# Two delta-rule attentions of a long kernel: the products with W give way to a product and a subtraction ahead of the inverse

## The chip, the cores and the metric

The kernel runs on one core of one Trainium2 chip. The metric is the device time of one execution in microseconds (us), taken as the median of several runs. TensorE (PE) multiplies matrices, VectorE (DVE) and ScalarE (ACT) do elementwise work, GpSimd (POOL) does small powers and indirect transfers, and SyncE (SP) issues transfers. Each engine works through its own instructions in order and waits on semaphores for the others.

## The reference, cut to what matters

The whole program is eight stages in sequence (attention and feed-forward of four layers). Two of them hold a delta rule in chunks: the first stage, `l0_attn`, and the fifth, `l2_attn`. There are 8 sequences of 512 rows, 4 heads, and chunks of 128 rows in the kernel (the mathematics doesn't depend on the chunk). For each head and chunk of `l0_attn`:

```
inv   = (I + strictly_lower(kb @ k.T))^-1        # kb = k * beta, v is already v * beta
u     = inv @ v
w     = inv @ kb
u_adj = u - w @ S                                # S: the state, key columns x value columns
out   = q @ S + lower(q @ k.T) @ u_adj
S     = S + k.T @ u_adj
```

`l2_attn` is the same with a decay in each row: what it takes from the state (by k and by q) is multiplied by `from_start`, the decay since the start of the chunk, and S shrinks by `whole` from one chunk to the next. Its value columns are 64 a head (256 in all); in `l0_attn` they are 32 a head (128 in all).

## The kernel before, in words

All products are in f32. A matmul of f32 shows in the trace as two MATMUL records ("x2"), so four heads are "x8".

**Lanes.** Each stage takes its 8 sequences as units in two lanes, A (units 0, 2, 4, 6) and B (1, 3, 5, 7), so there are four rounds of A and B. A unit is cut into phases, the places of `yield` in the code, and each engine's program is written in one order by `weave`: a phase of A, then a phase of B, and so on, with A one phase ahead. No engine can change this order.

**Chunks and pairs.** A unit has four chunks of 128 rows, worked on as two pairs. For a pair, `score_pe` forms kb·k and q·k for all heads of both chunks (L782), and `levels_pe` builds the inverses from small blocks, level by level (L800, L808, L816, L825, L833; the last two are `left6`, L840, and `right6`, L847). After `right6` DVE writes the last block of the inverse (L926, the step `whole`). The transposed inverse of each head is XT, the masked q·k is AT.

**After the inverse, per pair.**

- phase `wt`: `wt_pe` forms the transposed W of both chunks, 8 matmuls with 32 output rows each (L934), and ACT moves them to SBUF with a minus sign (L941, `wt_moved`).
- phase `u` of a chunk: `values_pe` accumulates -W·S (one matmul, L947) and inverse·v of four heads (L949) in bank 1; behind it, a matmul of q with S (L1107 in `l0_attn`, L2664 in `l2_attn`). ACT copies bank 1 to U (L955, `values`). In `l2_attn` DVE scales q·S (L2886).
- phase `out` of a chunk: k.T·U into bank 3 (L1110, L2667; `added`), AT·U of four heads (L1112, L2671; `out`). DVE keeps the head blocks of bank 3 and adds them to S (L1330 and L1332; L2890 and L2892; `state`), ACT (`l0_attn`, L1198) or DVE (`l2_attn`, L2895) takes the output (`got`).

S is zero in chunk 0. Written by lane, the order of the phases at the end of pair 0 is:

```
A.right6 B.left6 A.wt B.right6 A.u0 B.wt A.out0 B.u0 A.u1 B.out0 A.out1 B.u1 (A's next) B.out1
```

Pair 1 has the same order, with chunks 2 and 3. In `l0_attn` A's next phase is the score of pair 1 (L782) or, after chunk 3, a transpose (L422); in `l2_attn` it is `between`, whose decays DVE prepares (L2865) for a product of PE (L2650), or the squares of the output (ACT L2766, DVE L2899).

**Filters in `l0_attn`.** Through the levels of pair 0, PE also forms a long convolution (L1249) in bank 1 of both lanes, and DVE copies it out in eight copies (L1278, mark `filtered`). DVE has them in its order by phases: the last four behind A's `whole` and ahead of B's `whole`. PE waits for the last of them before the values of chunk 0.

**Decay in `l2_attn`.** Before the pairs, DVE multiplies the rows `kb` by `from_start` (L2860) and `krow` by `to_end` (L2861), once a unit.

Of the kernel before, what the change touches and what calls it, by code (L numbers as in the profile page):

```python
# [7 lines left out]
ALU = mybir.AluOpType  # L8
# [3 lines left out]
P = 128  # L12
# [676 lines left out]
HEADS, DK = 4, 32  # L689
# [51 lines left out]
def delta_phases(pair):  # L741

    names = [f"score{pair}"]
    for n in range(1, SMALL_LEVELS + 1):
        names += [f"left{pair}_{n}", f"right{pair}_{n}"]
    names += [f"turn{pair}", f"left{pair}_6", f"right{pair}_6", f"wt{pair}"]
    for chunk in (2 * pair, 2 * pair + 1):
        names += [f"u{chunk}", f"out{chunk}"]
    return names


class Delta:
# [5 lines left out]
    def __init__(self, c, arena, dv, scaled):  # L758
        self.c, self.dv, self.width = c, dv, HEADS * dv
        self.NT, self.AT, self.X, self.XT, self.T1 = (arena.take(2, HEADS, P) for _ in range(5))  # L760
        self.WT = arena.take(2, P)
# [12 lines left out]
        self.qS = arena.take(HEADS, dv) if scaled else None  # L774
# [155 lines left out]
    def wt_pe(self, pe, u, pair, kbe):  # L930
        for j in range(2):
            pe.wait_ge(*u.dve.at(f"whole{pair}"))
            for hh in range(HEADS):
                made = pe.matmul(u.banks[0][DK * hh:DK * hh + DK, cols_of(j)], chunk_heads(kbe, 2 * pair + j)[:, hh, :],  # L934
                                 self.XT[:, j, hh, :])
        made.then_inc(*u.pe.step(f"wt{pair}"))
        yield f"wt{pair}"

    def wt_act(self, act, u, pair):
        act.wait_ge(*u.pe.at(f"wt{pair}"))  # L940
        act.mul(flat(self.WT), u.banks[0][:, 0:2 * P], -1.0).then_inc(*u.act.step(f"wt_moved{pair}"))  # L941
        yield f"wt{pair}"

    def values_pe(self, pe, u, j, vb):

        bank, dv = u.banks[1], self.dv
        pe.matmul(bank[:, 0:self.width], self.WT[:, j, :], self.S, start=True, stop=False)  # L947
        for hh in range(HEADS):
            made = pe.matmul(bank[:, hh * dv:(hh + 1) * dv], self.XT[:, j, hh, :], vb[:, hh, :], start=False,  # L949
                             stop=hh == HEADS - 1)  # L950
        return made

    def values_act(self, act, u, chunk):
        act.wait_ge(*u.pe.at(f"u{chunk}"))
        act.copy(all_heads(self.U[chunk % 2]), u.banks[1][:, 0:self.width]).then_inc(*u.act.step(f"values{chunk}"))  # L955
# [59 lines left out]
class L0Attn:  # L1015
# [39 lines left out]
    def pe(self, pe, u):  # L1055
# [31 lines left out]
        for pair in range(CHUNKS // 2):  # L1087
# [8 lines left out]
            yield from d.wt_pe(pe, u, pair, m.kb)  # L1096
            for j in range(2):
                chunk = 2 * pair + j
                pe.wait_ge(*u.act.at(f"wt_moved{pair}"))
                if chunk > 0:  # L1100
                    pe.wait_ge(*u.dve.at(f"state{chunk - 1}"))
# [4 lines left out]
                d.values_pe(pe, u, j, chunk_heads(m.vb, chunk)).then_inc(*u.pe.step(f"u{chunk}"))  # L1106
# [41 lines left out]
    def act(self, act, u):  # L1148
# [36 lines left out]
        for pair in range(CHUNKS // 2):  # L1185
# [7 lines left out]
            yield from d.wt_act(act, u, pair)  # L1193
            for chunk in (2 * pair, 2 * pair + 1):
                d.values_act(act, u, chunk)
# [85 lines left out]
    def dve(self, dve, u):  # L1281
# [36 lines left out]
        for pair in range(CHUNKS // 2):  # L1318
# [7 lines left out]
            yield f"wt{pair}"  # L1326
            for chunk in (2 * pair, 2 * pair + 1):
                yield f"u{chunk}"
# [1251 lines left out]
class L2Attn:  # L2580
# [16 lines left out]
    def pe(self, pe, u):  # L2597
# [47 lines left out]
        for pair in range(CHUNKS // 2):  # L2645
# [9 lines left out]
            yield from d.wt_pe(pe, u, pair, m.kb)  # L2655
            for j in range(2):
                chunk = 2 * pair + j
                pe.wait_ge(*u.act.at(f"wt_moved{pair}"))
                if chunk > 0:
                    pe.wait_ge(*u.dve.at(f"state{chunk - 1}"))  # L2660
                else:
                    pe.wait_ge(*u.dve.at("cleared"))
                d.values_pe(pe, u, j, chunk_heads(m.vrow, chunk, L2_ATTN_DV)).then_inc(*u.pe.step(f"u{chunk}"))
# [30 lines left out]
    def act(self, act, u):  # L2694
# [54 lines left out]
        for pair in range(CHUNKS // 2):  # L2749
# [10 lines left out]
            yield from d.wt_act(act, u, pair)  # L2760
            for chunk in (2 * pair, 2 * pair + 1):
                d.values_act(act, u, chunk)
# [29 lines left out]
    def dve(self, dve, u):  # L2792
# [67 lines left out]
        dve.tensor_tensor(heads_of(m.kb), heads_of(m.kb), over(m.from_start, DK), ALU.mult).then_inc(*u.dve.step())  # L2860
        dve.tensor_tensor(heads_of(m.krow), heads_of(m.krow), over(m.to_end, DK), ALU.mult).then_inc(*u.dve.step("weighed"))  # L2861
        yield "keys"
        for pair in range(CHUNKS // 2):
# [18 lines left out]
            yield f"wt{pair}"  # L2882
            for chunk in (2 * pair, 2 * pair + 1):
                dve.wait_ge(*u.pe.at(f"carried{chunk}"))
# [973 lines left out]
```

## Time and profile before

| | |
|---|---|
| median of 3 runs | 6054.68 us (6027.5, 6054.68, 6063.11) |
| profiled execution | 6045.51 us, span 6044.2 us |
| mean granted TensorE clock | 0.736 of full speed |
| busy, share of the span | PE 70%, PE weight loads 54%, DVE 50%, ACT 32%, POOL 14% |
| chain that ended last, by engine | PE 50%, DVE 29%, ACT 12%, issue 4% |

The profiled execution took 1.3 us more than its span, and lies 9.2 us under the median. The page cuts the span into 40 equal slices of 151 us: `l0_attn` lies in slices 1 to 7 and `l2_attn` in slices 20 to 27.

### The profile page before, as it was taken

What the parts mean: (1) busy time and instruction counts of PE and PEld (TensorE: products, weight loads), DVE (VectorE), ACT (ScalarE), POOL (GpSimd) and SP (SyncE); (2) the same over time, 40 slices, a digit from 0 to 9 for tenths busy, and PEclk for the clock granted to TensorE, in tenths of its full rate; (3) what the DMA queues carried; (4) which work ended last, traced back from release to release, by engine and by line L of the source; (5) the groups of instructions that cost most, each with busy time, mean ns of one, the idle gap of its engine ahead of it and who ended that gap; (6) DMA issues with size and microseconds to landing.
All of it is one profiled execution on the core that took longest, in us unless ns stands there. A gap on an engine that the chain in (4) does not pass through costs nothing.

```text
span 6044.2 us, 94874 instructions
## 1 busy us (share of the span) xinstructions
PE 4245.8 (70%) x39740; PEld 3259.7 (54%) x39740; DVE 2998.6 (50%) x7965; ACT 1939.8 (32%) x4236; POOL 817.7 (14%) x600
## 2 busy tenths in 40 slices
PE   6686968468878887855475766757767677766298
PEld 5574847345555565544364655634444445445277
DVE  4445363335555555565446455455565555555333
ACT  2233132223333333311323233234444444442122
POOL 0000000231110111124200000011111111110443
PEclk6555555588888888866666666568887788778599
DMA  9100000240000000011200000000000000000255
GB/s 260 40 2 1 2 1 2 76 128 1 1 1 1 1 1 1 1 35 19 48 2 1 1 1 1 2 1 1 1 1 1 1 1 1 1 1 1 66 162 141
DMA packets 140860, 152.33 MB, mean 25 GB/s; under 512 B 7808, under 2 KB 128002, under 8 KB 139792
## 3 DMA queue, kind: packets, MB, share of 16 engines
q1 hardware_dynamic: 119024, 128.21, 7.4%
q0 software_dynamic: 21408, 18.05, 1.8%
q8 instruction: 313, 5.13, 0.4%
q14 instruction: 115, 0.94, 0.1%
HBM read 87.38 MB, written 59.76 MB: 24 GB/s over the span
## 4 chain that ended last, share of the span: by engine, by line
PE 50%; DVE 29%; ACT 12%; issue 4%; POOL 2%; DMA 1%; another core or an unknown queue 1%; SPq 0%; DVEq 0%; POOLq 0%; ACTq 0%
PE banks_lane L800 4%; ACT work L3226 4%; PE banks_lane L422 3%; PE banks_lane L3663 2%; PE banks_lane L1882 2%; PE banks_lane L3068 2%; PE banks_lane L1249 2%; PE banks_lane L808 2%; PE banks_lane L3112 2%; DVE weights L3319 1%; PE banks_lane L949 1%; ACT work L1976 1%; PE banks_lane L3147 1%; DVE work L2789 1%; PE banks_lane L1940 1%
## 5 line engine op out<-in xcount | busy, mean ns | idle before, releaser
L422 PE MATMUL banks_lane<-constants,work 128*128 128x128 f32 x968 | 202.2, 358 | 513.8 <-DVE work L408 231.5
L422 PEld LDWEIGHTS banks_lane<-constants,work 128*128 128x128 f32 x968 | 155.1, 186 | 587.2 <-DVE work L408 222.8
L402 POOL TENSOR_TENSOR weights<-weights,constants 128x4 f32<-128x4 f32 x76 | 78.5, 1033 | 2126.7 <-DVE weights L397 2126.7
L422 PE MATMUL banks_lane<-constants,weights 128*128 128x128 f32 x596 | 124.2, 347 | 339.1 <-DVE weights L408 99.0
L3226 ACT ACTIVATE work<-banks_lane,weights 128x192 f32<-128x192 f32 (+1 forms) x512 | 248.2, 498 | 245.8 <-DVE weights L3323 245.8
L422 PEld LDWEIGHTS banks_lane<-constants,weights 128*128 128x128 f32 x596 | 88.5, 178 | 372.2 <-issue 172.6
L3331 POOL TENSOR_TENSOR weights<-weights,constants 128x16 f32<-128x16 f32 x64 | 185.4, 2896 | 530.9 <-DVE weights L3239 530.9
L402 POOL TENSOR_TENSOR work<-work,constants 128x4 f32<-128x4 f32 x76 | 77.3, 1018 | 1199.2 <-DVE work L397 1199.2
L3147 PE MATMUL banks_lane<-constants,work 128*128 128x128 f32 x896 | 149.7, 316 | 120.0 <-DVE work L3311 70.5
L3147 PEld LDWEIGHTS banks_lane<-constants,work 128*128 128x128 f32 x896 | 113.2, 160 | 149.9 <-DVE work L3311 89.0
L2029 DVE TENSOR_REDUCE work<-banks_lane 128x2 f32<-128x512 f32 x256 | 158.9, 684 | 68.0 <-PE banks_lane L1896 67.8
L3319 DVE TENSOR_REDUCE weights<-banks_lane 128x2 f32<-128x384 f32 (+1 forms) x256 | 122.1, 519 | 113.7 <-PE banks_lane L3134 113.3
L1976 ACT ACTIVATE work<-banks_lane 128x384 f32<-128x384 f32 (+1 forms) x256 | 118.5, 550 | 176.5 <-PE banks_lane L1917 108.5
L800 PE MATMUL banks_lane<-work 64*64 64x32 f32 x2048 | 124.2, 292 | 72.3 <-DVE work L890 68.6
L3075 PE MATMUL banks_lane<-constants,weights 128*128 128x128 f32 x256 | 68.6, 420 | 137.8 <-DVE weights L3250 81.5
L800 PEld LDWEIGHTS banks_lane<-work 64*64 64x64 f32 x2048 | 115.0, 220 | 78.2 <-DVE work L890 70.3
L3663 PE MATMUL banks_lane<-weights,work 128*128 128x256 f32 x624 | 145.4, 387 | 15.2 <-DVE weights L3705 15.2
L3162 PE MATMUL banks_lane<-work 128*64 128x128 f32 x1792 | 128.0, 284 | 34.1 <-ACT work L3188 34.1
L656 POOL DMA_INDIRECT out<-weights,chunk_places x78 | 121.5, 1557 | 197.2 <-DVE chunk_places L648 135.2
L569 POOL DMA_INDIRECT room_l_ffn<-weights,indices x96 | 92.7, 965 | 403.0 <-DVE weights L392 347.6
L3068 PE MATMUL banks_lane<-weights,work 128*128 128x512 f32 x192 | 143.5, 909 | 0.0
L1882 PE MATMUL banks_lane<-weights,work 128*128 128x128 f32 x1024 | 134.0, 295 | 5.9 <-ACT work L1998 5.9
(779 smaller groups left out, 11169.5 us busy)
## 6 DMA issues: line engine op xcount, KB each, us to landing
work<-experts_dram_l_ffn SPq DMA_DIRECT2D x39, 964.0 KB
room_l_ffn<-work SPq DMA_DIRECT2D x30, 1188.0 KB, 15.4
work<-experts_dram_l_ffn SPq DMA_DIRECT2D x23, 512.0 KB
weights<-weights_dram SPq DMA_DIRECT2D x1, 4833.5 KB, 14.0
work<-room_l_ffn SPq DMA_DIRECT2D x36, 132.0 KB, 3.3
weights<-weights_dram SPq DMA_DIRECT2D x1, 4112.0 KB, 12.8
weights<-bands_dram SPq DMA_DIRECT2D x1, 4096.0 KB, 13.1
weights<-room_l_ffn SPq DMA_DIRECT2D x26, 132.0 KB, 4.5
```

The costliest lines, as they stand in the source:

```text
L402: pool.tensor_tensor(n.rstd, n.rstd, c("neghalf", cols=(0, n.rstd.shape[1])), ALU.pow).then_inc(*u.pool.step(name))
L422: done = pe.transpose(bank[0:rows, t * P:(t + 1) * P], block, c("ident"))
L800: made = pe.matmul(b[2][g, m * SMALL:(m + 1) * SMALL], self.strict[g, m, :], self.x[g, m, :])
L1882: made = pe.matmul(b[1][:, cols_of(t)], m.ff[:, f, cols_of(t)], self.w(u, f"down{f}"), start=f == 0, stop=f == L1_ATTN_FF - 1)
L1976: act.activation(m.probs[:, hh, 0:blocks, :].rearrange("p b q -> p (b q)"), b[hh][:, 0:blocks * P], ACT.Exp, scale=L1_ATTN_SCALE).then_inc ...
L2029: dve.tensor_reduce(m.top[r][:, :, hh, L1_ATTN_HD], b[hh][:, :].rearrange("p (t c) -> p t c", t=2), AX, ALU.max, negate=True).then_inc(*u. ...
L3068: pe.matmul(b[n][:, :], m.xT[:, cols_of(t)], self.w(u, "qkv", cols=(n * L2_FFN_INNER, (n + 1) * L2_FFN_INNER))).then_inc(*u.pe.step(f"proj ...
L3147: made = pe.transpose(u.banks[2 + side][:, cols_of(hh)], m.probs[n % 2][:, hh, side * P:(side + 1) * P], self.c("ident"))
L3226: act.activation(m.probs[n % 2][:, hh, L2_FFN_BACK + lo:2 * P], u.banks[side][:, j * span:(j + 1) * span], ACT.Exp, scale=m.q_factor[:, t, ...
L3319: dve.tensor_reduce(m.top[:, t, 4 * group + side:4 * group + 4:2], u.banks[side][:, 0:2 * span].rearrange("p (j c) -> p j c", j=2), AX, AL ...
L3331: pool.tensor_tensor(m.rn[:, t, :, :], m.rn[:, t, :, :], c("neghalf", cols=(0, 2 * L2_FFN_HEADS)).rearrange("p (n h) -> p n h", n=2), ALU. ...
L3663: made = pe.matmul(bank[:, g * CHUNK:(g + 1) * CHUNK], self.w(u, f"{name}{f}", cols=(g * P, (g + 1) * P)), m.z[:, f, :], start=f == 0, sto ...
```

## The change

The products with W go. Instead, `carry_pe` multiplies kb of the chunk with S (one matmul, with `kbq[:, chunk, 0, :]`, the transposed kb that the scores already use), DVE subtracts the result from the values in place, and the inverse is applied once to what is left. Chunk 0 has no carry, since S is zero there. The result of the inverse goes to the upper half of bank 1. In `l2_attn` DVE takes two instructions, one to scale by `from_start` and one to subtract, and the scaling of `kb` ahead of the pairs (L2860) goes. The new phase `carry` stands ahead of `u` in chunks 1 to 3, and `wt` is gone:

```
A.right6 B.left6 A.u0 B.right6 A.out0 B.u0 A.carry1 B.out0 A.u1 B.carry1 A.out1 B.u1 (A's next) B.out1
A.right6 B.left6 A.carry2 B.right6 A.u2 B.carry2 A.out2 B.u2 A.carry3 B.out2 A.u3 B.carry3 A.out3 B.u3 (A's next) B.out3
```

```diff
-    def wt_pe(self, pe, u, pair, kbe):
...
-    def wt_act(self, act, u, pair):
...
-    def values_pe(self, pe, u, j, vb):
-
-        bank, dv = u.banks[1], self.dv
-        pe.matmul(bank[:, 0:self.width], self.WT[:, j, :], self.S, start=True, stop=False)
+    def carry_pe(self, pe, u, chunk, kbq):
+
+        pe.wait_ge(*u.dve.at(f"state{chunk - 1}"))
+        pe.matmul(u.banks[1][:, 0:self.width], kbq[:, chunk, 0, :], self.S).then_inc(*u.pe.step(f"carry{chunk}"))
+
+    def values_pe(self, pe, u, chunk, vb):
+
+        pe.wait_ge(*u.dve.at(f"whole{chunk // 2}"))
+        if chunk > 0:
+            pe.wait_ge(*u.dve.at(f"rest{chunk}"))
         for hh in range(HEADS):
-            made = pe.matmul(bank[:, hh * dv:(hh + 1) * dv], self.XT[:, j, hh, :], vb[:, hh, :], start=False,
-                             stop=hh == HEADS - 1)
+            made = pe.matmul(self.made(u)[:, hh * self.dv:(hh + 1) * self.dv], self.XT[:, chunk % 2, hh, :], vb[:, hh, :])
+        made.then_inc(*u.pe.step(f"u{chunk}"))
+
+    def made(self, u):
+        return u.banks[1][:, self.width:2 * self.width]
...
@@ l0_attn, pe
-            yield from d.wt_pe(pe, u, pair, m.kb)
             for j in range(2):
                 chunk = 2 * pair + j
-                pe.wait_ge(*u.act.at(f"wt_moved{pair}"))
                 if chunk > 0:
-                    pe.wait_ge(*u.dve.at(f"state{chunk - 1}"))
+                    d.carry_pe(pe, u, chunk, m.kbq)
+                    yield f"carry{chunk}"
                     pe.wait_ge(*u.act.at(f"got{chunk - 1}"))
...
@@ l0_attn, dve
-            yield f"wt{pair}"
             for chunk in (2 * pair, 2 * pair + 1):
+                if chunk > 0:
+                    rest = chunk_heads(m.vb, chunk)
+                    dve.wait_ge(*u.pe.at(f"carry{chunk}"))
+                    dve.tensor_tensor(rest, rest, of_heads(b[1], d.width, DK), ALU.subtract).then_inc(*u.dve.step(f"rest{chunk}"))
+                    yield f"carry{chunk}"
                 yield f"u{chunk}"
...
@@ l2_attn, dve
-        dve.tensor_tensor(heads_of(m.kb), heads_of(m.kb), over(m.from_start, DK), ALU.mult).then_inc(*u.dve.step())
...
-            yield f"wt{pair}"
             for chunk in (2 * pair, 2 * pair + 1):
+                if chunk > 0:
+                    rest, part = chunk_heads(m.vrow, chunk, d.dv), d.gain.rearrange("p (h d) -> p h d", d=d.dv)
+                    dve.wait_ge(*u.pe.at(f"carry{chunk}"))
+                    dve.wait_ge(*u.dve.last())
+                    dve.tensor_tensor(part, of_heads(b[1], d.width, d.dv),
+                                      over(m.from_start[:, chunk * HEADS:(chunk + 1) * HEADS], d.dv), ALU.mult).then_inc(*u.dve.step())
+                    dve.wait_ge(*u.dve.last())
+                    dve.tensor_tensor(rest, rest, part, ALU.subtract).then_inc(*u.dve.step(f"rest{chunk}"))
+                    yield f"carry{chunk}"
                 dve.wait_ge(*u.pe.at(f"carried{chunk}"))
```

The PE and ACT programs of `l2_attn` change in the same way as those of `l0_attn`.

## Rows read from the trace of the kernel before

**Rows 1.** The page's 40 slices: PE's busy tenths and its granted clock.

```profile
PE   6686968468878887855475766757767677766298
PEclk6555555588888888866666666568887788778599
```

**Rows 2.** Chain that ended last, `l0_attn`, pair 0: start, length in us, what.

```profile
146.51 1.01 PE banks_lane L934 x16
147.52 1.90 PE banks_lane L847 x16
149.41 0.72 PE banks_lane L947 x2
150.14 1.55 PE banks_lane L949 x8
151.68 0.59 PE banks_lane L1107 x2
...
153.28 0.73 PE banks_lane L1110 x2
...
155.56 0.59 PE banks_lane L947 x2
...
158.28 0.43 PE banks_lane L947 x2
...
167.66 2.01 PE banks_lane L782 x14
```

**Rows 3.** The same chain at pair 1: first product of W, and A's next phase.

```profile
213.83 1.01 PE banks_lane L934 x16
...
234.98 0.85 PE banks_lane L422 x4
```

**Rows 4.** Timeline of DVE and ACT in `l0_attn`: start us, us, instruction, idle before.

```profile
145.81 1.77 DVE L1278 COPY weights<-banks_lane 64x256 f32<-64x256 f32 x4
154.05 0.29 DVE L1330 TENSOR_TENSOR work<-banks_lane,constants 128x128 f32<-128x128 f32 x1 [3.91 <-PE banks_lane L1110]
...
151.72 0.27 ACT L955 COPY weights<-banks_lane 128x128 f32<-128x128 f32 x1 [3.75 <-PE banks_lane L949]
```

**Rows 5.** Chain that ended last, `l2_attn`, pair 0 of the first round.

```profile
3075.05 1.01 PE banks_lane L934 x16
...
3077.95 1.15 PE banks_lane L947 x2
3079.11 1.60 PE banks_lane L949 x8
3080.70 0.96 PE banks_lane L2664 x2
...
3086.50 0.43 PE banks_lane L947 x2
3086.93 0.84 PE banks_lane L949 x8
...
3092.70 0.43 DVE work L2886
```

**Rows 6.** The same chain, pair 1: its first product of W, and its end.

```profile
3150.48 1.01 PE banks_lane L934 x16
...
3167.48 0.37 ACT work L955
```

**Rows 7.** Timeline of DVE in `l2_attn`: the scaling of one chunk's q·S.

```profile
3086.54 0.42 DVE L2886 TENSOR_TENSOR work<-banks_lane,work 128x256 f32<-128x256 f32 x1 [1.39 <-PE banks_lane L2664]
```

**Rows 8.** Chain that ended last, `l2_attn`, ahead of the first scores.

```profile
3023.34 0.69 DVE work L2860
```

**Rows 9.** Stretches: us, length, busy of PE, PEld, DVE, ACT, POOL; PEclk, DMA share, GB/s.

```profile
3084.00:3093.00 9.00, 8.66 (x63) 7.90 (x61) 4.75 (x12) 1.12 (x3) 0.00 (x0) 1.00 0.00 0
...
3410.00:3425.00 15.00, 15.00 (x89) 12.41 (x88) 2.86 (x6) 2.09 (x5) 0.00 (x0) 0.50 0.00 1
...
146.00:168.00 22.00, 22.00 (x135) 20.49 (x137) 3.92 (x11) 3.22 (x10) 0.00 (x0) 0.50 1.06 244
```

More of the change, by code:

```diff
@@ L745, in delta_phases @@
         names += [f"left{pair}_{n}", f"right{pair}_{n}"]
-    names += [f"turn{pair}", f"left{pair}_6", f"right{pair}_6", f"wt{pair}"]
+    names += [f"turn{pair}", f"left{pair}_6", f"right{pair}_6"]
     for chunk in (2 * pair, 2 * pair + 1):
-        names += [f"u{chunk}", f"out{chunk}"]
+        names += ([f"carry{chunk}"] if chunk > 0 else []) + [f"u{chunk}", f"out{chunk}"]
     return names
@@ L760, in __init__ @@
         self.NT, self.AT, self.X, self.XT, self.T1 = (arena.take(2, HEADS, P) for _ in range(5))
-        self.WT = arena.take(2, P)
         small, whole = INVERTED * SMALL, lambda v: v.rearrange("p c h n -> p (c h n)")
@@ L928, in levels_dve @@
         yield f"right{pair}_6"
-    def wt_pe(self, pe, u, pair, kbe):
[L931 to L936, printed above, removed]
-        yield f"wt{pair}"
-    def wt_act(self, act, u, pair):
-        act.wait_ge(*u.pe.at(f"wt{pair}"))
-        act.mul(flat(self.WT), u.banks[0][:, 0:2 * P], -1.0).then_inc(*u.act.step(f"wt_moved{pair}"))
-        yield f"wt{pair}"
-    def values_pe(self, pe, u, j, vb):
-        bank, dv = u.banks[1], self.dv
-        pe.matmul(bank[:, 0:self.width], self.WT[:, j, :], self.S, start=True, stop=False)
+    def carry_pe(self, pe, u, chunk, kbq):
[5 more added lines that the diff above has]
+            pe.wait_ge(*u.dve.at(f"rest{chunk}"))
         for hh in range(HEADS):
-            made = pe.matmul(bank[:, hh * dv:(hh + 1) * dv], self.XT[:, j, hh, :], vb[:, hh, :], start=False,
-                             stop=hh == HEADS - 1)
-        return made
+            made = pe.matmul(self.made(u)[:, hh * self.dv:(hh + 1) * self.dv], self.XT[:, chunk % 2, hh, :], vb[:, hh, :])
+        made.then_inc(*u.pe.step(f"u{chunk}"))
+    def made(self, u):
+        return u.banks[1][:, self.width:2 * self.width]
     def values_act(self, act, u, chunk):
         act.wait_ge(*u.pe.at(f"u{chunk}"))
-        act.copy(all_heads(self.U[chunk % 2]), u.banks[1][:, 0:self.width]).then_inc(*u.act.step(f"values{chunk}"))
+        act.copy(all_heads(self.U[chunk % 2]), self.made(u)).then_inc(*u.act.step(f"values{chunk}"))
 L0_ATTN_SHORT, L0_ATTN_LONG, L0_ATTN_CONV = 5, 64, 4
@@ L1105, in pe @@
                     pe.wait_ge(*self.first(u).dve.at("filtered"))
-                d.values_pe(pe, u, j, chunk_heads(m.vb, chunk)).then_inc(*u.pe.step(f"u{chunk}"))
+                d.values_pe(pe, u, chunk, chunk_heads(m.vb, chunk))
                 pe.matmul(b[2][:, 0:P], m.kbq[:, chunk, 1, :], d.S, start=True, stop=False)
@@ L1192, in act @@
             yield from d.levels_act(act, u, pair)
-            yield from d.wt_act(act, u, pair)
             for chunk in (2 * pair, 2 * pair + 1):
+                if chunk > 0:
+                    yield f"carry{chunk}"
                 d.values_act(act, u, chunk)
@@ L1325, in dve @@
             yield from d.levels_dve(dve, u, pair, filters)
-            yield f"wt{pair}"
             for chunk in (2 * pair, 2 * pair + 1):
+                if chunk > 0:
[3 more added lines that the diff above has]
+                    yield f"carry{chunk}"
                 yield f"u{chunk}"
@@ L2654, in pe @@
             yield from d.levels_pe(pe, u, pair, iter(()))
-            yield from d.wt_pe(pe, u, pair, m.kb)
             for j in range(2):
                 chunk = 2 * pair + j
-                pe.wait_ge(*u.act.at(f"wt_moved{pair}"))
                 if chunk > 0:
-                    pe.wait_ge(*u.dve.at(f"state{chunk - 1}"))
+                    d.carry_pe(pe, u, chunk, m.kbq)
+                    yield f"carry{chunk}"
                 else:
                     pe.wait_ge(*u.dve.at("cleared"))
-                d.values_pe(pe, u, j, chunk_heads(m.vrow, chunk, L2_ATTN_DV)).then_inc(*u.pe.step(f"u{chunk}"))
+                d.values_pe(pe, u, chunk, chunk_heads(m.vrow, chunk, L2_ATTN_DV))
                 pe.matmul(b[2][:, 0:d.width], m.kbq[:, chunk, 1, :], d.S).then_inc(*u.pe.step(f"carried{chunk}"))
@@ L2759, in act @@
             yield from d.levels_act(act, u, pair)
-            yield from d.wt_act(act, u, pair)
             for chunk in (2 * pair, 2 * pair + 1):
+                if chunk > 0:
+                    yield f"carry{chunk}"
                 d.values_act(act, u, chunk)
@@ L2881, in dve @@
             yield from d.levels_dve(dve, u, pair, iter(()))
-            yield f"wt{pair}"
             for chunk in (2 * pair, 2 * pair + 1):
+                if chunk > 0:
+                    rest, part = chunk_heads(m.vrow, chunk, d.dv), d.gain.rearrange("p (h d) -> p h d", d=d.dv)
[5 more added lines that the diff above has]
+                    dve.tensor_tensor(rest, rest, part, ALU.subtract).then_inc(*u.dve.step(f"rest{chunk}"))
+                    yield f"carry{chunk}"
                 dve.wait_ge(*u.pe.at(f"carried{chunk}"))
```

## The prediction

> **What bounds the kernel now.** I read the page's slices first [rows 1]. The two stages that the change touches, slices 1 to 7 and 20 to 27, show PE at 6 to 9 tenths busy and mostly at a granted clock of 5 or 6 tenths, so PE's products cost most where they stand in them. The chain that ended last then tells whether the phases behind the inverse belong to the part where PE sets the pace. In `l0_attn` it runs from A's first product of W at 146.51 to A's next score at 167.66 through PE alone, one group ending where the next begins [rows 2]; the same at pair 1, from 213.83 to 234.98 [rows 3]. Both are 21.15 us long. In `l2_attn` it is PE alone from 3075.05 to 3092.70, 17.65 us, and from 3150.48 to 3167.48, 17.00 us [rows 5, 6]. So what is taken from PE in these stretches comes off the time, and a wait put into them comes on top, unless PE has the other lane's work for it. There are 4 rounds of each: the products of W begin 5.76 us apart in the two lanes in every pair of `l0_attn` and 6.62 us apart in every pair of `l2_attn`, so one round stands for four.
>
> The granted clock is the other thing to read. `l0_attn` has 0.50 through the whole stretch [rows 9]. `l2_attn` begins at 0.50 and goes to 1.00 within it [rows 9]. In 6 of the 8 stretches it rises 7.6 to 8.8 us after A's first product of W; in two it rises only about 14.2 us after it, though PE was busy all the time (one of them is the 15 us row at 0.50).
>
> **The sum for `l0_attn`.** I write the new order down with the lengths of the rows. From [rows 2]: `right6` 1.90; inverse·v 1.55; q·S 0.59; k.T·U with AT·U 0.43 + 1.55 = 1.98 behind a large product and 0.73 + 1.55 = 2.28 behind small tiles; the carry is the product of L947, with another stationary operand of the same size, 0.43 behind a product of 128 columns and 0.72 behind small tiles. A first product behind small tiles costs 0.13 more (0.72 against 0.59).
>
> Pair 0. A.u0 now stands where A.wt stood, at 146.51, but it waits for `filtered`, and DVE's last copies end at 147.58 [rows 4]; before, W products and `right6` of B covered that wait. With 0.06 for the hand-over it starts at 147.64: 1.13 us of new wait, with B.right6 queued behind it. Then A.u0 1.68 + 0.59, B.right6 1.90, A.out0 2.28, B.u0 2.14, A.carry1 0.43, B.out0 1.98, A.u1 2.14, B.carry1 0.43, A.out1 1.98, B.u1 2.14: end 165.33, not 167.66. Gain 2.33 us. It is made of 2.02 for the two phases `wt`, 1.31 for the product with the zero state in chunk 0, minus the wait of 1.13, and 0.13 of smaller gaps.
>
> Pair 1: A.carry2 0.72, B.right6 1.90, A.u2 2.27, B.carry2 0.43, A.out2 1.98, B.u2 2.14, A.carry3 0.43, B.out2 1.98, A.u3 2.14, B.carry3 0.43, A.out3 1.98, B.u3 2.14: 18.54 us, not 21.15. Gain 2.61.
>
> What the new round trip costs: behind each carry stands PE -> DVE -> PE. The new subtraction is of the size of L1330, 0.29 us [rows 4], with about 0.1 for both hand-overs 0.4. PE has the other lane's `out` in between, 1.98 us, so it is hidden; if that cover were gone, it would cost 0.4 for each of 24 carries, 10 us. The state is added at the end of the same kind of wait (two DVE instructions, 0.6 us) behind AT·U and the other lane's `u`, over 3 us. The copy of U (0.27) has q·S and the other lane's phase. ACT loses the move of W, which nothing follows. Four rounds: 4 x 4.94 = 19.8 us.
>
> **The sum for `l2_attn`.** Lengths at the low clock [rows 5]: inverse·v 1.60, q·S 0.96, k.T·U 1.15 behind small tiles and else, as the carry, 0.86 (twice the 0.43 at the high clock), AT·U 1.60. At the high clock 0.84, 0.49, 0.43, 0.84. The high one takes 0.52 of the time.
>
> Pair 0 wholly at the low clock: A.u0 2.75, B.right6 1.90, A.out0 2.75, B.u0 2.56, then carry 0.86, out 2.46, u 2.56, carry 0.86, out 2.46, u 2.56: 21.7 us. If the clock rises r us into it, it takes r + 0.52 x (21.7 - r). With r = 8.3 as before, 15.3, a gain of 2.4. With r = 14.2, 18.1, a loss of 0.45. Never: a loss of 4.1. What stands ahead of the rise changes most here: chunk 0 loses its product of 256 columns and `right6` with its small tiles moves in between the large products. So I take the middle, r = 11.25: 16.7, a gain of 1.0. Pair 1 wholly low, up to inverse·v of B.u3: 1.15 + 1.90 + 2.75 + 0.86 + 2.46 + 2.56 + 0.86 + 2.46 + 2.56 + 0.86 + 2.46 + 1.60 = 22.5. Large products stand there as early as before, so r = 8.3: 15.7, a gain of 1.3; never, a loss of 5.5.
>
> On the release of the clock the Trainium skill ("TensorE: Matmul & The Clock Gate", section "What's actually happening") says that it is a matter of how long TensorE has been busy, not of how many matmuls were issued. By that rule alone r in pair 0 would be 8.3 + 1.75 (the new place of the first large product behind `right6`, 4.65 against 2.90 us), the gain 1.5, and the whole sum 2 us larger. The two stretches with the late rise, busy from their start, speak for not leaning on it.
>
> DVE has more to do here: two instructions a carry, the first of the form of L2886, 0.42 [rows 7], the second at least 0.29 [rows 4] and at most 0.69, a tensor_tensor of twice the columns [rows 8]; I take 0.42, nearest in size. With the hand-overs 1.0 us. The cover is the other lane's `out`, at the high clock 0.43 + 0.84 = 1.27: hidden, with 0.2 to 0.3 to spare. In that window DVE is the next engine: 4.75 of 9.0 us before [rows 9], and 4 more instructions in a round of both lanes' chunks, about 1.8 us. In order, DVE does rest of A, gain and state of B, q·S of A, rest of B; each of PE's waits still ends before the other lane's phase does. If nothing covered it, 24 x 1.0 = 24 us.
>
> The scaling of kb goes (L2860): 0.69 at first sight, but the next instruction takes over its longer start, so 0.6; for unit B it lies on the chain [rows 8], for unit A it is followed by idle time. So one a round.
>
> Together 1.0 + 1.3 + 0.6 = 2.9 a round, 11.6 us in four. No transfer is issued or moved, and the carry's operand is already in SBUF for the scores.
>
> **Forecast.** 19.8 + 11.6 = 31 us less. Against the profiled execution, 6045.5 (its span and 1.3), that is 6014; against the median of the runs, which lies 9.2 higher, 6023 us, 0.5% less. The bounds of the clock alone make it 24 to 37 us.
>
> **The rivals.**
>
> *The clock stays low in `l2_attn` (slower).* Place: the stretches behind the inverse; W's products and chunk 0's product with S, which stood just ahead of the rise, are gone. Price, if none of the 8 rises: 4 x (4.1 + 5.5 - 0.6) = 36 us lost, 19.8 won, +16: 6071. It decides the sign from about 5 or 6 stretches on (31 us against 6 us for each that doesn't rise). For it: `l0_attn`, with the same order and smaller products, never rises [rows 9], and two of eight rose late. Against: the later chunks keep all their products of 256 columns.
>
> *DVE's round trip is not covered.* Then 10 + 24 = 34 us come back: 6057, no change. For it: a spare of only 0.2 us in `l2_attn`. Against: 1.5 us to spare in `l0_attn` and at the low clock. Part of it, in `l2_attn` alone, makes 6035 to 6047.
>
> *The clock rises in `l0_attn` too.* From `right6` of B on, the stretch is 13.5 us without small tiles or W. If it rose some 5.4 us into that, as in `l2_attn`, 8 us would run at the high clock and save 3.7 us a stretch, 30 in eight, with the next scores 37: 5986. Against: today's stretch has 14.4 us behind B's W and more products of 128 columns in it, and stays at 0.50 [rows 9].
>
> *The change saves nothing in `l0_attn` because A.u0 waits.* The wait would have to be 4.9 us a round; DVE's copies bound it at 1.13. It only counts within the range.
>
> **Chances.** Forecast 0.76, the clock staying low 0.08, the uncovered round trip 0.09, the rise in `l0_attn` 0.07. The range leaves the ends of the outer cases out and adds what single runs scatter (6027.5 to 6063.11): 5998 to 6064. A change under about 1% can't be told from none for this kernel. Below 5994: 0.09; above 6115: 0.03; within: 0.88.
>
> **What the profile after would show.** L934, L941 and L2860 gone; each of the pairs' stretches in `l0_attn` 18.5 to 18.8 us long and still PE from end to end; in pair 0 one wait of PE of 1.1 us for L1278 ahead of A.u0; no idle time of PE ahead of the values of chunks 1 to 3; in `l2_attn` the clock rising at 8 to 14 us, and the stretches 15.3 to 18 us. Wrong would be idle time of PE between carry and values, or windows of `l2_attn` at 0.50 to their end. The prediction as a whole would be wrong if phases ahead of these stretches, which the change doesn't touch, came out with another clock.

## The result, and the profile after

The changed kernel takes 6004.13 us (median of 8 runs, 5995.76 to 6012.26), the kernel before 6041.58 us on the same chips (8 runs, 6027.5 to 6063.11): a ratio of 0.9939, with a 95% interval of 0.9925 to 0.9952, so 37 us (29 to 45) less. A second comparison later gave 0.9947 (0.9933 to 0.9960), 32 us. The forecast was 31 us less, 6023 us from the median of 6054.68 known then; from the median of the eight runs, 6041.58, the same 31 us would give 6011. So 13 of the 19 us between 6023 and 6004 lie in where the kernel before was put, and 6 in the change.

The page's slices after [rows 1] show the same picture, a little shorter:

```profile
span 5997.2 us, 93854 instructions
...
PE   6686968468788888855475666857777677776298
...
PEclk6555555688889888876766666668887788778599
```

The chain that ended last in pair 0 of `l0_attn`, which answers to [rows 2]; L940 is inverse·v, L1099 q·S, L1102 and L1104 k.T·U and AT·U, L932 the carry, L1271 a copy of the filter:

```profile
147.43 0.44 DVE weights L1271
147.87 0.04 issue
147.91 1.92 PE banks_lane L940 x8
149.83 0.59 PE banks_lane L1099 x2
150.42 1.90 PE banks_lane L846 x16
152.31 0.72 PE banks_lane L1102 x2
153.04 1.55 PE banks_lane L1104 x8
154.58 1.71 PE banks_lane L940 x8
...
156.88 0.43 PE banks_lane L932 x2
157.30 0.43 PE banks_lane L1102 x2
...
166.26 2.02 PE banks_lane L781 x15
```

and pair 1, for [rows 3]:

```profile
212.79 0.72 PE banks_lane L932 x2
...
231.94 0.85 PE banks_lane L422 x4
```

The timeline of the same stretch, PE and DVE, with the idle time before each:

```profile
147.91 1.92 PE L940 MATMUL banks_lane<-work,weights 128*128 128x32 f32 x8 [1.13 <-DVE weights L1271]
...
157.34 0.29 DVE L1323 TENSOR_TENSOR work<-work,banks_lane 128x128 f32<-128x128 f32 x1 [3.65 <-PE banks_lane L932]
```

One wait of PE is new, 1.13 us ahead of A.u0, for DVE's copies of the filter. Everywhere else PE goes on without a gap: the carry is 0.43 us, DVE's subtraction starts behind it and ends at 157.63, 1.65 us before the inverse needs it at 159.28 (B's k.T·U and AT·U, 0.43 + 1.55 us, stand in between). Pair 0 takes 166.26 - 147.91 + 1.13 = 19.48 us, not 21.15; pair 1 takes 19.15, not 21.15. All four rounds repeat these lengths to 0.02 us.

In `l2_attn`, for [rows 5] and [rows 6] (L2660 q·S, L2663 and L2667 the two products with U):

```profile
3050.70 1.90 PE banks_lane L940 x8
...
3059.91 0.96 PE banks_lane L2660 x2
3060.87 0.85 PE banks_lane L932 x2
3061.72 0.85 PE banks_lane L2663 x2
3062.58 1.35 PE banks_lane L2667 x8
3063.93 0.89 PE banks_lane L940 x8
...
3068.43 0.42 DVE work L2890
...
3123.93 1.15 PE banks_lane L932 x2
...
3139.66 0.37 ACT work L948
```

Stretches of the changed kernel, as in [rows 9] (PEclk is the third number from the end):

```profile
3050.70:3062.50 11.80, 11.80 (x53) 10.31 (x52) 3.57 (x8) 1.33 (x3) 0.00 (x0) 0.50 0.00 0
3064.50:3068.40 3.90, 3.89 (x27) 3.33 (x26) 2.42 (x6) 0.75 (x2) 0.00 (x0) 1.00 0.00 0
3123.90:3131.50 7.60, 7.60 (x35) 6.29 (x34) 2.69 (x6) 0.95 (x2) 0.00 (x0) 0.50 0.00 0
3132.50:3139.60 7.10, 7.10 (x54) 6.79 (x54) 5.30 (x14) 0.74 (x2) 0.00 (x0) 1.00 0.00 0
...
213.00:232.00 19.00, 19.00 (x96) 18.64 (x96) 3.60 (x11) 2.27 (x8) 0.00 (x0) 0.50 0.00 1
```

Pair 0 went from 17.65 to 17.73 us (3050.70 to 3068.43): it saves nothing in this round, since the clock rises 12.8 us into it and not 8.7. Pair 1 went from 17.00 to 15.73. Ahead of the scores, the chain behind ACT now meets one multiplication and then the next step (L2870); before, L2861 (0.60 us) stood behind L2860. That is 0.6 us less, as forecast [rows 8]:

```profile
3000.20 0.69 DVE work L2857
3000.90 0.33 DVE weights L2870
```

The phases between these stretches, which the change leaves as they were, also came out with another clock. From the end of pair 0's stretch to the start of pair 1's in the first round, before and then after, and a part of it after:

```profile
3093.90:3150.40 56.50, 43.29 (x1010) 36.80 (x1010) 26.00 (x63) 12.03 (x27) 0.00 (x0) 0.56 0.01 2
```

```profile
3069.60:3123.90 54.30, 40.88 (x1011) 35.01 (x1011) 26.00 (x63) 11.93 (x27) 0.00 (x0) 0.63 0.01 3
3084.10:3090.80 6.70, 3.12 (x113) 2.43 (x112) 4.10 (x12) 2.21 (x5) 0.00 (x0) 1.00 0.01 2
```

The columns are those of [rows 9]. The clock is high once more, in the scores of pair 1; in the kernel before, the window from 3101.0 to 3158.5 shows 0.50 throughout.

### The profile page after: what moved, and what is told of

Read it like the earlier page. It is cut to its first block, busy times and chain, and to the rows that moved or that the text cites. A ratio compares the mean times of both kernels' runs of the same rounds, so it can differ in the third digit from the quotient of the medians.

```text
span 5997.2 us, 93854 instructions
## 1 busy us (share of the span) xinstructions
PE 4198.1 (70%) x39196; PEld 3226.0 (54%) x39196; DVE 3018.7 (50%) x8029; ACT 1929.0 (32%) x4204; POOL 816.5 (14%) x600
## 4 chain that ended last, share of the span: by engine, by line
PE 49%; DVE 30%; ACT 12%; issue 3%; POOL 3%; DMA 2%; another core or an unknown queue 1%; SPq 0%; DVEq 0%; POOLq 0%; ACTq 0%
PE banks_lane L799 4%; ACT work L3230 4%; PE banks_lane L422 3%; PE banks_lane L3667 2%; PE banks_lane L1879 2%; PE banks_lane L3072 2%; PE banks_lane L1242 2%; PE banks_lane L807 2%; PE banks_lane L3116 2%; PE banks_lane L940 2%; DVE weights L3323 1%; PE banks_lane L3151 1%; ACT work L1973 1%; DVE work L2786 1%; PE banks_lane L1924 1%
## 5 line engine op out<-in xcount | busy, mean ns | idle before, releaser
L422 PE MATMUL banks_lane<-constants,work 128*128 128x128 f32 x968 | 199.5, 354 | 507.2 <-DVE work L408 230.9
L422 PEld LDWEIGHTS banks_lane<-constants,work 128*128 128x128 f32 x968 | 152.3, 183 | 581.6 <-DVE work L408 221.9
L422 PE MATMUL banks_lane<-constants,weights 128*128 128x128 f32 x596 | 125.5, 349 | 339.2 <-DVE weights L408 97.0
L422 PEld LDWEIGHTS banks_lane<-constants,weights 128*128 128x128 f32 x596 | 89.3, 179 | 374.9 <-issue 178.2
L3079 PE MATMUL banks_lane<-constants,weights 128*128 128x128 f32 x256 | 68.1, 417 | 139.0 <-DVE weights L3254 81.8
## 6 DMA issues: line engine op xcount, KB each, us to landing
room_l_ffn<-work SPq DMA_DIRECT2D x30, 1188.0 KB, 15.1
weights<-bands_dram SPq DMA_DIRECT2D x1, 4096.0 KB, 13.2
```

The lines of the kernel that those rows point to most:

```text
L422: done = pe.transpose(bank[0:rows, t * P:(t + 1) * P], block, c("ident"))
```

## The experiments

Lengths of stretches are read from the chain, from the end of `left6` of B to A's next phase (line numbers of the kernel before): the first product L782, L422 or L2650, or ACT's squares L2766. In `l2_attn` this end lies behind DVE's work, so pair 0 measures 18.8 and pair 1 17.4 in the kernel before. The time at the low clock in a stretch is added up from windows of 0.5 us. In `l0_attn` all four rounds are alike; in `l2_attn` the four rounds stand in order:

```
kernel          l0_attn pair 0/1   l2_attn pair 0              low clock                pair 1                      low clock
before          21.15 / 21.15      18.82 21.46 18.89 18.78     8.7 14.2  8.8  8.6       17.40 20.43 17.74 17.32     8.4 14.6  9.1  8.2
changed         19.48 / 19.15      18.90 18.42 18.09 18.82    12.8 11.8 11.2 12.7       16.12 16.08 16.55 15.85     7.9  7.8  8.8  7.3
l0_only         19.48 / 19.15      18.63 18.59 19.12 21.74     8.3  8.2  9.3 14.7       17.68 20.44 17.78 20.58     8.9 14.7  9.2 14.9
l2_only         21.15 / 21.15      18.71 18.61 18.63 18.14    12.4 12.2 12.3 11.3       16.04 16.37 15.65 16.09     7.7  8.4  6.9  7.8
after_again     19.48 / 19.15      18.64 18.64 18.64 18.30    12.3 12.3 12.3 11.6       16.21 15.89 16.22 16.43     8.1  7.4  8.1  8.5
gap_both        18.85 / 19.15      18.72 18.78 18.55 19.04    12.0 12.1 11.7 12.6       16.29 15.66 16.30 16.39     8.2  6.9  8.2  8.4
slow_rest       19.48 / 19.15      19.63 19.91 19.64 19.64    11.8 13.2 12.7 11.8       18.40 18.21 18.26 18.31     9.0  8.3  8.7  8.8
early_filters   18.28 / 19.15      18.50 19.11 18.57 18.61    12.0 13.3 12.1 12.2       16.51 15.87 16.21 18.47     8.7  7.3  8.1 12.7
keep_zero       19.48 / 19.15      19.38 19.48 19.36 20.86    12.0 12.2 12.0 15.1       15.76 16.37 18.80 16.13     7.1  8.4 13.4  7.9
no_zero         20.30 / 21.16      17.95 17.99 17.87 21.42     8.7  8.8  8.5 15.9       17.40 20.24 20.28 17.52     8.4 14.2 14.3  8.6
wake_l2         19.48 / 19.15      16.30 16.09 15.85 19.77     5.5  5.0  4.5 12.8       16.17 15.64 16.37 16.45     8.0  6.9  8.4  8.6
```

### The two halves by themselves

`l0_only` has the change in `l0_attn` and the old code, with W, in `l2_attn`; `l2_only` the other way round. Each keeps both versions of the class:

```diff
+class DeltaW:                       # the class of before, with wt_pe, wt_act and the old values_pe
...
-        self.norm, self.delta = Norm(arena), Delta(c, arena, L2_ATTN_DV, True)
+        self.norm, self.delta = Norm(arena), DeltaW(c, arena, L2_ATTN_DV, True)
```

> The change in l0_attn alone; l2_attn keeps W. Theory (PE sets the pace, what is taken from PE comes off the time): each pair's stretch of l0_attn shorter by 1.7 and 2.0 us as in the changed kernel, 14.7 us in eight stretches, so a ratio of 0.9976 to the kernel before; the stretches of l2_attn as long as before, 17.0 to 20.3 us by when the clock rises. Rival (most of the 37 us comes from the granted clock in l2_attn and elsewhere, by chance or by the change): under 8 us here, and the rest with the change in l2_attn alone.

> The change in l2_attn alone; l0_attn keeps W. Theory: the stretch of pair 1 shorter by 1.3 us, that of pair 0 by 0 to 2 us depending on when the clock rises, 0.6 us a round for the scaling of kb: 8 to 14 us, ratio 0.9977 to 0.9987. Rival (the change raises the granted clock beyond its own stretches, in the phases between them): 20 us or more, ratio 0.9967 or lower, with a higher granted clock in the stretches from one decay product to the next.

`l0_only` measured 0.9979 (0.9967 to 0.9990), 12.7 us; `l2_only` 0.9976 (0.9962 to 0.9989), 14.5 us. The halves give about the same, and the medians speak for both theories; the intervals (6 to 20 us, and 7 to 23) reach into the rivals' figures (under 8, and 20 or more). In `l0_only` the stretches have the lengths of the changed kernel (14.7 us less in the eight), and the three late rises in its `l2_attn` hide 3.7 us of that from its own profile.

The sign that was named for the rival of `l2_only` is there in part. Between pair 0 and pair 1 of `l2_attn` the granted clock was 0.56 in all eight cases of the kernel before and `l0_only`. In the changed kernel, `after_again` and `l2_only` it was 0.62 or 0.63 in 11 of 12 cases. In the profiles the whole stage `l2_attn` takes 1045.0 and 1045.9 us in the first two and 1018.7, 1018.0 and 1024.4 in the other three, 25 us less on the mean. Some 14 of them are in the stretches and 2.4 were forecast for the scaling; the other 9 or so lie in phases that the sum put at nothing. `no_zero` below has W and yet 0.63 or 0.64 there (its stage takes 1032.6 us), and `keep_zero` has no W and 0.55 or 0.56 in three of four, so W alone doesn't set it. Each profile is one execution, the timing of `l2_only` gives less than 25 us, and what moves the clock in these phases stays open.

### The changed kernel again

> The changed kernel again, as the partner of the others on this chip. The sum of the two halves measured by themselves (0.9979 and 0.9976) is 0.9955; the first comparison gave 0.9939 (0.9925 to 0.9952). Theory (the halves don't act on each other): 0.9945 to 0.9955. Rival (together they save more than apart): 0.9939 or less. The stretches of l0_attn 19.47 and 19.15 us again; in l2_attn the clock rises after 11 to 13 us in pair 0 and after 7 to 9 us in pair 1, in none after 14 us.

Measured 0.9947, with an interval (0.9933 to 0.9960) that holds both the product of the halves (0.9955) and the first comparison. So no interplay of the halves is needed to explain it. Its stretches agree with those of the first profile to within about 0.6 us.

### A slower round trip

```diff
...
+                    for _ in range(2):
+                        dve.tensor_tensor(spare, rest, of_heads(b[1], d.width, DK), ALU.subtract).then_inc(*u.dve.step())
+                        dve.wait_ge(*u.dve.last())
                     dve.tensor_tensor(rest, rest, of_heads(b[1], d.width, DK), ALU.subtract).then_inc(*u.dve.step(f"rest{chunk}"))
```

and in `l2_attn` the scaling three times, not once.

> The changed kernel with two more DVE instructions in each round trip from carry to values (results unchanged): 0.66 us more in l0_attn, 0.92 us more in l2_attn. Theory (the round trip is hidden behind the other lane's out, with 1.5 us to spare in l0_attn and at the low clock, 0.2 to 0.3 us at the high one): l0_attn the same to 1 us, no idle PE ahead of the values; in l2_attn about 0.7 us of idle PE ahead of each of the 14 or so values at the high clock, 10 us (5 to 20) in all. Rival (the round trip already ends the wait): 24 x 0.66 + 24 x 0.92 = 38 us more.

Measured 0.9977 (0.9963 to 0.9991), 0.003 to 0.004 above the changed kernel. In `l0_attn` nothing moves, 19.48 and 19.15 again. In `l2_attn` the stretches are 152.0 us in sum, 13.2 more than in the changed kernel. The chain shows how it goes over DVE, and the timeline how long PE stands still:

```profile
3068.06 0.45 PE banks_lane L932 x2
3068.50 0.02 issue
3068.53 0.43 DVE work L2889
...
3068.99 0.43 DVE work L2889
...
3069.44 0.43 DVE work L2892
...
3069.90 0.44 DVE work L2895
...
3070.38 1.10 PE banks_lane L940 x8
```

```profile
3066.47 1.10 PE L940 MATMUL banks_lane<-work,weights 128*128 128x64 f32 x8 [0.17 <-DVE work L2895]
...
3070.38 1.10 PE L940 MATMUL banks_lane<-work 128*128 128x64 f32 x8 [0.62 <-DVE work L2895]
```

0.92 us more of DVE give 0.62 us of idle PE at the high clock: the spare was 0.3 us. In sum PE stands idle 8.2 us ahead of the values in `l2_attn`, and the values behind such a wait take 1.10 us and not 0.89. In the changed kernel PE has no idle time ahead of any value of chunks 1 to 3, so the round trip is covered there, and in `l2_attn` barely.

### The wait for the filters

Two ways to take it away. `gap_both` puts an empty phase where `wt` stood (in pair 0 of both stages), so that right6 of B comes first again:

```diff
             yield from d.levels_pe(pe, u, pair, products)
+            if pair == 0:
+                yield f"gap{pair}"
```

> The changed kernel with an empty phase in pair 0 where wt stood, in both stages, so that right6 of B comes before u0 of A again. Theory on the wait for the filters: in l0_attn right6 of B runs while DVE ends its copies, PE's idle 1.13 us ahead of A's values of chunk 0 goes, 4.5 us in four rounds. Theory on the clock in l2_attn: the large products of pair 0 stand together from 1.9 us on instead of from 4.7 us, so the clock rises 8 to 10 us into the stretch instead of about 13, 1.5 to 2.5 us less a round. Together 10 to 14 us under the changed kernel, ratio 0.9915 to 0.9922 to the kernel before. Rival (the rise doesn't depend on where right6 stands): only the 4.5 us. Rival 2 (without the other lane's phase between u0 and out0 the copy of U is exposed): 0.3 us a stretch more, nothing gained in l2_attn.

Measured 0.9942 (0.9923 to 0.9961), the same as the changed kernel. In `l0_attn` the 1.13 us are gone, but pair 0 is only 0.63 us shorter, because another wait took its place:

```profile
145.79 0.02 issue
145.81 0.59 ACT work L879
146.41 0.04 issue
146.45 1.97 PE banks_lane L848 x16
```

B.right6 needs ACT's copy of B.left6, and nothing stands between the two products any more. W's products had covered that copy too, and so does A.u0 in the changed kernel. In `l2_attn` the same wait of 0.65 us appears, and nothing is gained: the clock still rises at about 12 us. So moving `right6` back doesn't bring the early rise back.

`early_filters` leaves the phases and takes larger groups of filter products, so that all the copies end ahead of A's `whole`:

```diff
-L0_ATTN_GROUP, L0_ATTN_WAIT = 6, 17
+L0_ATTN_GROUP, L0_ATTN_WAIT = 7, 15
```

> The changed kernel with groups of 7 products for the long filter (19 groups, not 22) and DVE's copies two phases earlier, so that all eight stand ahead of whole of A. The order of the phases stays. Theory: PE's wait of 1.13 us ahead of A's values of chunk 0 goes with nothing in its place, since u0 of A still covers ACT's copy for right6 of B: the pair 0 stretch of l0_attn 18.3 to 18.4 us (19.47 before), 4.5 us in four rounds, 0.0007 of the ratio, which is at the edge of what timing can tell. Rival: the longer groups of filter products push the levels of pair 0 back and the stretch gains what the levels lose.

The stretch takes 18.28 us, 1.2 less, and PE has no wait in it. From one round's stretch to the next, 258.1, 258.8 and 259.1 us pass, against 260.4, 259.5 and 259.4 in `after_again` (measured from the last product of B.left6 in the one and, in the other, from the end of A.right6, the same in each round), 3.3 us less in three rounds where 3.6 are saved in the stretches, so the levels give back little. Timed, it gave 0.9961 (0.9947 to 0.9975) beside 0.9947, 9 us more by the medians, and the two intervals overlap: timing shows no gain from it. In its profile the `l2_attn` stretches, which it leaves alone, are 2.8 us longer than in `after_again`, with one rise of pair 1 at 12.7 us; scatter of this kind is as large as the gain looked for.

### What delays the clock in `l2_attn`

`no_zero` is the kernel before without the product with the zero state, in both stages; `keep_zero` the changed kernel with that product kept in `l2_attn`, its result unused.

```diff
-        pe.matmul(bank[:, 0:self.width], self.WT[:, j, :], self.S, start=True, stop=False)
+        if chunk > 0:
+            pe.matmul(bank[:, 0:self.width], self.WT[:, j, :], self.S, start=True, stop=False)
```

```diff
+                    pe.matmul(b[1][:, 0:d.width], m.kbq[:, 0, 0, :], d.S)
                 d.values_pe(pe, u, chunk, chunk_heads(m.vrow, chunk, L2_ATTN_DV))
```

> The kernel before with only the product with the zero state in chunk 0 left out; W stays. Theory: the pair 0 stretches of l0_attn 0.9 us shorter (0.72 and 0.59 less, 0.16 and 0.24 more for the first product behind small ones), pair 1 unchanged at 21.15; in l2_attn the clock of pair 0 rises at about 12 us and the stretch doesn't get shorter. Rival: the clock rises at 8.7 us as before and the l2_attn stretch of pair 0 is 1.4 us shorter, which would put the late rise down to W's products.

> The changed kernel, but in l2_attn the product with the zero state in chunk 0 is kept as a matmul whose result is not used, ahead of the values. Theory (the late rise of the clock in pair 0, at 12 instead of 8.7 us, comes from the loss of that product ahead of it): the low clock lasts 8 to 9 us in pair 0 again and the stretch is 18.4 us or less although it holds 1.4 us more work. Rival (it comes from the loss of the W products, or from the place of right6): low clock for 12 to 13 us and a stretch of 19.6 us.

My theory falls in both. `no_zero` keeps the rise at 8.5 to 8.8 us in three of four and saves 0.9 us there; in the fourth it rises only at 15.9 us. `keep_zero` leaves it at 12 us or later and lengthens the stretch (timed 0.9961, 0.9947 to 0.9975). What the kernels with the rise at about 8.7 us (before, `l0_only`, `no_zero`) have in common is W. The part of `no_zero` in `l0_attn` came as expected: 20.30, 0.85 us less. There is a single execution of `no_zero`, so it shows lengths but no difference in time.

The chains show what stood before each rise (an ordering in the trace, not by itself a cause). In the kernel before it is q·S of A, W of B, k.T·U of A, one behind the other. In the changed kernel `right6` of B, with its small tiles, stands in W's place, and the rise comes behind the next such run: q·S of B, carry1 of A, k.T·U of B (3059.91 to 3062.58 above). In pair 1 that run comes early (q·S of A, carry2 of B, k.T·U of A), and so does the rise. But such a run isn't enough: in the eight stretches with W where the clock was low for 14 us or more, the same run stood in its place and no rise came. In one and the same order the rise also scatters by 2 us from round to round, so the moment at which a stretch begins may count as well; no run separates that. `wake_l2` lengthens the first run, with one matmul of 512 columns that nobody reads:

```diff
                 pe.matmul(b[2][:, 0:d.width], m.kbq[:, chunk, 1, :], d.S).then_inc(*u.pe.step(f"carried{chunk}"))
+                if u.lane == 0 and chunk == 0:
+                    pe.matmul(b[0][:, :], m.kT[:, chunk, :], flat(m.kT))
```

> The changed kernel; in l2_attn, lane A, pair 0, one matmul of 512 columns is added behind q.S of chunk 0 (1.9 us of added work at the low clock), its result not read. In all profiles of kernels without W so far the clock rose in pair 0 behind the run q.S of B, carry1 of A, k.T.U of B (about 2.7 us of large products), 12 us into the stretch; with W, behind q.S of A, W of B, k.T.U of A, at 8.7 us. Theory (it is such an unbroken run of large products that it takes, and the change has broken the first one): with the added product the clock rises at 5 to 8 us, the stretch is 18.4 us or less. Rival (W's own products or something else bring it): 12 to 14 us at the low clock, the stretch 20 us.

In three of four rounds the clock rises at 4.5 to 5.5 us and the stretch takes 15.9 to 16.3 us, 2.4 less, with more work in it; in the fourth it rises at 12.8 us and the stretch takes 19.8. Timed 0.9923 (0.9903 to 0.9943). `wake_both` and `wake_early` below hold the same addition, and there the rise comes at 4.6 to 6.0 us in two rounds of four each, and at 12.8 to 13.3 in the others. So the addition brings the rise forward in 7 stretches of 12, to a place where none of the 24 stretches of pair 0 without W or added products has it; why the other five miss it is open. Whether a run of small products of the same length would do the same was not tried.

### The low clock in `l0_attn`

```diff
                 pe.matmul(b[2][:, 0:P], m.kbq[:, chunk, 1, :], d.S, start=True, stop=False)
+                if u.lane == 0 and j == 0:
+                    for _ in range(2):
+                        pe.matmul(b[0][:, :], m.kT[:, chunk, :], flat(m.kT))
```

> The changed kernel; in l0_attn, lane A alone, two matmuls of 512 columns are added behind q.S of chunks 0 and 2, with a result that nobody reads (3.8 us of added work at the low clock). It measures what the low clock costs in these stretches, the third rival of the prediction. If a longer run of large products raises the clock there and it stays up: low clock for about 5 to 8 us and then 1.00, the stretches 17 to 20 us instead of 19.5 and 19.15, so none to 2 us less each although they hold 3.8 us more. If the products of 32 columns let it fall again or it doesn't rise: 23 us each, 30 us more in all.

Measured 0.9897 (0.9878 to 0.9915), another 0.004 to 0.005 under the changed kernel. The chain of pair 0 in the first round:

```profile
148.87 3.04 PE banks_lane L1102 x4
151.92 1.07 PE banks_lane L846 x16
152.99 0.42 PE banks_lane L1105 x2
153.41 0.81 PE banks_lane L1107 x8
154.22 0.89 PE banks_lane L940 x8
```

```profile
152.00:160.50 8.50, 8.50 (x84) 8.27 (x83) 2.92 (x9) 1.58 (x6) 0.00 (x0) 1.00 1.06 253
```

L1102 is the added work. Behind it every product takes about half its time (inverse·v 0.89 for 1.71, AT·U 0.81 for 1.55, right6 1.07 for 1.90). In the third and fourth round of pair 0 and the first and second of pair 1, though, the clock falls again after a few us and the stretch takes 20.0 and 19.6 us, 0.5 longer than in the changed kernel. The eight stretches are 12.3 us shorter in sum (142.2 and 154.5), though they hold 3.0 to 3.4 us more work each; the scores behind pair 0 gain too where the clock is still high (L781 1.07 us, not 2.02).

### Put together

`wake_both` has both additions, `wake_early` the early filters as well.

> The changed kernel with the added large products of both stages. If the two act independently, 0.9897 and 0.9923 against 0.9947 and 0.9939 of the changed kernel alone: about 1.4 times 0.003 less, 0.987 to 0.989, faster than both kernels. Rival (single profiles caught lucky places of the rise): 0.991 or more.

> The same with the filter's copies two phases earlier as well. Theory: PE's wait ahead of A's values of chunk 0 is gone, 4.5 us in four rounds, 0.9865 to 0.988. Rival (the wait was where the low clock stood anyway, and the rise moves with it): no difference to wake_both.

0.9890 (0.9872 to 0.9908), 5957.59 us, and 0.9871 (0.9850 to 0.9891), 5948.58 us, with the kernel before at 6026.26. Both beat both kernels; against each other they aren't told apart. The two additions together are not told apart from that of `l0_attn` by itself (0.9897), so what `wake_l2` adds to it stays open. Their stretches, as in the table above:

```
kernel       l0_attn pair 0            low clock            l0_attn pair 1            low clock            l2_attn pair 0            low clock
wake_l0      15.28 15.36 20.03 20.01    6.2  6.3 16.6 16.6   19.64 19.64 16.25 16.04   16.2 16.2 8.8 8.4   (nothing added)
wake_both    15.27 15.40 15.41 20.02    6.2  6.4  6.4 16.6   19.64 16.72 15.48 15.94   16.2  9.9 7.2 8.1   19.79 20.01 16.48 16.11   13.0 13.3 5.9  5.1
wake_early   21.69 13.78 15.07 13.82   21.7  4.4  7.2  4.5   15.57 16.71 16.72 16.24    7.4  9.9 9.9 8.8   15.88 20.00 16.50 19.86    4.6 13.3 6.0 13.0
```

The addition in `l0_attn` raised the clock in 23 of these 24 stretches (in one of `wake_early` it never rose), and in six of them it fell again early on. So the gain is one of many stretches together and not of each.

## Why the prediction was right

**What bounds it.** That PE sets the pace behind the inverse, and that work taken from it comes off the time, is borne out in `l0_attn` and, for the stretches that the sum covers, in `l2_attn`.

**`l0_attn`, forecast 19.8 us, measured 14.7 in the profile and 12.7 by itself.** The mechanism and the wait for the filters (1.13 us, to the hundredth) were right. The term that was mis-sized is the length of inverse·v, put down at 1.55, and at 1.68 behind small tiles. The 1.55 is its length behind the large product W·S. In the new order it follows the products of 32 columns of AT·U and takes 1.71; behind the wait for the filters it takes 1.92 and behind right6 1.84, not 1.68. In [rows 2] W·S itself carried those 0.16 us (0.59 behind AT·U, 0.43 behind q·S); I took them off with it, in eight places a round: 1.3 us, 5.1 in four. `no_zero` shows the same lengths with W in place: 1.84 behind right6, 1.71 behind AT·U and 1.55 behind W·S.

**`l2_attn`, forecast 11.6 us, measured 14.5 by itself.** For six kernels without W and without added products (changed, `l2_only`, `after_again`, `gap_both`, `slow_rest`, `early_filters`) pair 1's rise was forecast at 8.3 us and seen at 6.9 to 9.0 in 23 of 24 stretches; that and the 0.6 us for the scaling were right. For pair 0 I took 11.25 us, the middle between two values, and it is 11.2 to 13.3, 12.2 on the mean, which by the same sum is a gain of 0.5 us a round and not 1.0. The reason given doesn't hold: neither chunk 0's product (`no_zero`, `keep_zero`) nor `right6` moving in by itself (`gap_both`) makes the difference. That it is W of B leaving the run of large products fits all profiles, but was not tried by itself. What made up for it is a term that the sum didn't have: with W, 8 of 24 stretches of three profiles (before, `l0_only`, `no_zero`) have the clock low for 14 us or more (2 of 8 in the profile before), without W none of the 48 of those six kernels does; `keep_zero` has one of 15.1 us. I had priced the late rise only as a risk of the change, and compared with stretches that rise early. Taken over two profiles each side, the eight stretches went from 152.7 us (150.8 and 154.6) to 138.9 (138.8 and 139.0), 14 us, and 2.4 for the scaling. The phases between the stretches add some 9 us in the profiles, which the sum had at nothing; the prediction itself named another clock there as a sign that it would be wrong as a whole. So that the total came out close is in part luck: `l0_attn` gave 5 us less than its sum, and `l2_attn` made it good through late rises and phases that the sum didn't price.

Three smaller points of the working. The six early rises were read at 7.6 to 8.8 us, the clock of the same profile gives 8.2 to 9.1, and 8.6 on the mean in place of 8.3. The bounds of the clock give 26 to 37 us from the sum's own terms (31.4 less 4 x 1.45, and more 4 x 1.4), not 24 to 37. And a change under 1% can be told from none here: the interval of the first comparison is 0.9925 to 0.9952.

**Where the rest of the profiled difference lies.** The two profiled executions differ by 6045.51 - 5998.48 = 47 us, 10 more than the medians; the stages between `l0_attn` and `l2_attn`, which the change doesn't touch, account for 5 of it. `l0_attn` as a whole takes 1056.1 us and not 1073.0, `l2_attn` 1018.7 and not 1045.0, so 26 us of the 47 lie in `l2_attn` and 17 in `l0_attn`.

**The rivals.** The round trip of DVE is covered, shown by `slow_rest`. The clock staying low in `l2_attn` didn't come. In pair 0 it rose at 11.2 to 13.3 us in the 24 stretches of the six kernels. The rule of the Trainium skill ("TensorE: Matmul & The Clock Gate", section "What's actually happening") goes by how long TensorE has been busy. The 10 us worked out in the prediction go by the place of a large product instead, so they don't follow from that rule, and that they are nearer than 8.3 says nothing for it. The traces don't agree with busy time alone: PE was busy without a gap at 0.50 for 14 us and more in eight stretches of `l2_attn`, and for 19 us in pair 1 of `l0_attn`. The clock doesn't rise in `l0_attn` by the change alone, and `wake_l0` shows what it is worth where it does and lasts: 15.28 us and not 19.48, 4.2 less with 3.04 us of added work. The products behind the addition take 8.60 us and not 15.84, 0.54 of it. The prediction's price (8 us that shrink by 3.7) has the same factor.

## What to carry to other kernels

An operation that is taken away was also cover for others, and part of the work ahead of a rise of the clock. W's products stood between ACT's copy, DVE's copies and PE's next product; with them gone, the next late engine was DVE, and when that was mended by order alone it was ACT. Write the new order down with the row lengths, and take each length from a row with the same neighbour ahead of it. Where a part of the kernel stands at the low clock, look at what PE did before each rise before counting products saved as time saved.

## What the runs showed that I had not expected

Work that nobody needs made the kernel faster: 3.0 to 3.4 us of added products in each stretch of `l0_attn` gave 0.9897 against 0.9939 and 0.9947. It did so on the mean of an execution and not in every stretch. And a group of eight small products has no length of its own: inverse·v takes 1.55 (L949 of the kernel before), 1.71, 1.84 or 1.92 us (L940) at the same clock, by what stands before it.
